# Three of eight key chunks of P·V as products of fp16 halves

## The chip, the cores and the metric

One program runs on one core of a Trainium2 chip. Five engines work side by side and meet only at semaphores: PE (TensorE, the matmuls; its weight loads are listed apart as PEld), ACT (ScalarE), DVE (VectorE), POOL (GpSimd) and SP (SyncE, here only a queue of DMAs). The metric is the device time of one execution in microseconds; less is better.

## What is computed

The reference is one transformer layer on x of shape 4 x 1024 x 128, in fp32: differential attention, then a layer of sixteen gated experts that are mixed through an attention of their own. The change touches the first attention alone:

```python
q = (x @ Wq).reshape(B, T, 2 * H, D).transpose(0, 2, 1, 3) * scaling
dots = jnp.einsum('bhqd,bhkd->bhqk', q, k)
attn_w = jax.nn.softmax(dots.astype(jnp.float32), axis=-1)
attn_w = attn_w[:, :, 0] - lam * attn_w[:, :, 1]
attn = jnp.einsum('bhqk,bhkd->bhqd', attn_w, v)
```

There are 4 batches, 16 softmax heads of 32 columns in 8 pairs that share a V of 64 columns, and 1024 keys.

## The kernel before

The attention is cut into 128 **blocks**: one softmax head against 512 queries (half of a batch's). A **step** `j` has eight blocks (of one batch: four heads times two halves of the queries), so there are 16 steps; four blocks are a **group**. A block has eight **chunks** of 128 keys. For each chunk PE makes S^T = K^T Q in a bank of `st_ps` (three banks, `chunk`, L490, fp16 operands that carry the split parts), ACT takes the exponential into `pT` (L802, fp32), and for each block PE multiplies with V: 32 **units**, unit `n` being 128 queries against one chunk (`values`, L506). A unit is two fp32 matmuls, one for each half of the 128 queries (`TILE_COLS = 64`: the halves lie in different columns of the array), and the trace shows each of them as two passes, so a unit is four MATMUL records. V has a 65th column of ones, which gives the softmax's denominator.

Meanwhile PE computes ahead, through a ring of two pairs of PSUM banks (`ring_ps`), the row maxima of coming groups ("max", L553, emptied by DVE's reduction L1079), the projections of coming steps ("q", "k", "v"), and the transposes and output projection of finished groups ("cols", "project").

Each engine's order is written out. The outer loop is over `kb`; an iteration has eight **slots** `s`. In iteration `kb` PE works at the S chunks of block `kb` two chunks ahead (`ST_AHEAD = 2`), and at P·V of block `kb - 1`:

```python
c = 8 * kb + s + ST_AHEAD
chunk(c)                                   # pe.wait_ge(exp_ok, c - ST_BANKS + 1)
values(kb - 1, sum(PV_SHARE[:s]), sum(PV_SHARE[:s + 1]))   # PV_SHARE = (3, 4, 4, 4, 4, 4, 5, 4)
```

A "max" stands in slots 0, 2, 4 and 6 (in slot 0 ahead of P·V), "q", "k" and "v" at the end of slot 7 of three of a step's eight iterations. ACT does `exponentials(8 * kb + s)` in slot `s`; the first of a block waits until P·V of block `kb - 2` has freed the `pT` buffer (`pv_ok`), and just ahead of it ACT copies that block's sums out of `att_ps` (`raw_copy`, L810, which P·V of the next block waits for). So the chunk of PE's slot 1 waits for the block's first exponential, that of slot 2 for the second, that of slot 3 for the third. POOL combines the heads of a finished group (L386 to L411) and splits q and k of coming steps (L374, L376).

Of the kernel before, what the change touches and what calls it, by code (L numbers as in the profile page):

```python
# [55 lines left out]
SPLIT_PRODUCTS = ((0, 0), (0, 1), (1, 0))  # L56
# [48 lines left out]
EMPTIED = {engine: [emptied(engine, n) for n in range(len(RING) + 1)] for engine in "AV"}  # L105


def block_kernel(nc, x, wq, wkv, wout, lq1, lk1, lq2, lk2, gamma, sim, gates, eq, ek, ev, eo, out):
    ctx = ExitStack()
    with ctx:  # L110
        stack_of = {"memory": ctx}

        def sb(name, shape, dt=F32):
            return stack_of["memory"].enter_context(nc.sbuf_tensor(name, shape, dt))

        def ps(name, shape, dt=F32):
# [61 lines left out]
        st_ps = ps("st_ps", [P, ST_BANKS, HALF])  # L178
        att_ps = ps("att_ps", [P, HALF])
# [42 lines left out]
        weights_in, parts_set = sem("weights_in"), sem("parts_set")  # L222
        ring_ok, ring_A, ring_V = sem("ring_ok"), sem("ring_A"), sem("ring_V")
# [2 lines left out]
        shift_ok = sem("shift_ok")  # L226
        st_ok, exp_ok, pv_ok, raw_ok = sem("st_ok"), sem("exp_ok"), sem("pv_ok"), sem("raw_ok")
        recip_ok, tail_P = sem("recip_ok"), sem("tail_P")
        rms_const_ok = sem("rms_const_ok")
        e_v, e_p, e_a = sem("early_v"), sem("early_p"), sem("early_a")  # L230
        experts_in = sem("experts_in")
# [86 lines left out]
        def _(pool):  # L318
# [23 lines left out]

            pool.memset(v_sb[:, :, :, :, DV:DV1], 1.0).then_inc(parts_set, 1)
            pool.wait_ge(parts_set, 1)
            units = ka[:, :, :, :].rearrange("p a r t -> p (a r t)").bitcast(F32)
            pool.memset(units[K_MAX:K_ALL, :], PAIR_OF_ONE).then_inc(parts_set, 1)
            pool.wait_ge(parts_set, 2)
            pool.memset(units[K_MAX:K_MAX + 1, :], PAIR_OF_UNIT).then_inc(parts_set, 1)
            pool.wait_ge(parts_set, 3)

            def tokens(ap):
                return ap.unsqueeze(2).to_broadcast([P, NT, C])
# [62 lines left out]
            def early(b, stage):  # L415
# [9 lines left out]
                elif stage == 4:  # L425
                    pool.wait_ge(e_v, 8 * (b + 1))
                    pool.tensor_tensor(x2n[:, rows, :], x2c[:, :, :], tokens(gs[:, 0, rows]), ALU.mult).then_inc(g_nP, 1)

            for kb in range(FIRST_BLOCK, END_BLOCK):
                if (kb - 5) % 4 == 0 and 0 <= (kb - 5) // 4 < GROUPS:  # L430
                    combine((kb - 5) // 4)
                if (kb - 6) % 4 == 0 and 0 <= (kb - 6) // 4 < GROUPS:
                    rms((kb - 6) // 4)
                if (kb - 7) % 4 == 0 and 0 <= (kb - 7) // 4 < GROUPS:
                    normalize((kb - 7) // 4)
                for kind, lag in (("q", 13), ("k", 12)):
# [35 lines left out]
        def _(pe):  # L472
# [7 lines left out]
            def chunk(c):  # L480
# [6 lines left out]
                if c >= ST_BANKS:  # L487
                    pe.wait_ge(exp_ok, c - ST_BANKS + 1)
                for k0 in range(0, P, TILE_COLS):
                    mm = pe.matmul(st_ps[k0:k0 + TILE_COLS, c % ST_BANKS, :],  # L490
                                   ka[0:K_ALL, j % 2, r, kt * P + k0:kt * P + k0 + TILE_COLS],
                                   qa[0:K_ALL, j % 2, r, half * HALF:(half + 1) * HALF], start=True, stop=True)
                mm.then_inc(st_ok, 1)

            def values(blk, first, last):

                j, r = blk // 8, blk % 4
                for n in range(first, last):
# [6 lines left out]
                    for q0 in range(0, P, TILE_COLS):
                        mm = pe.matmul(att_ps[q0:q0 + TILE_COLS, qt * DV1:(qt + 1) * DV1],  # L506
                                       pT[:, blk % 2, kt, qt * P + q0:qt * P + q0 + TILE_COLS],
                                       v_sb[:, j % 2, kt, r // 2, :], start=kt == 0, stop=kt == 7)
                if last == 32:
                    mm.then_inc(pv_ok, 1)  # L510

# [64 lines left out]
            for kb in range(FIRST_BLOCK, END_BLOCK):  # L576
                for s in range(8):
                    c = 8 * kb + s + ST_AHEAD
                    if 0 <= c < CHUNKS:
                        if c == 0:  # L580
                            pe.wait_ge(parts_set, 3)
# [25 lines left out]
            for n in range(B):  # L607
# [3 lines left out]
                for t in range(NT):  # L611
                    mm = pe.transpose(gate_ps(n, t // 4)[:, t % 4 * P:(t % 4 + 1) * P], x2n[:, n * NT + t, :], ident[:, :])
# [148 lines left out]
        def _(act):  # L761
# [33 lines left out]
            def exponentials(c):  # L795
                blk, kt = divmod(c, 8)
                act.wait_ge(st_ok, c + 1)
                if c == 0:
                    act.wait_ge(ln_normed, B - 1)
                if kt == 0 and blk >= 2:  # L800
                    act.wait_ge(pv_ok, blk - 1)
                act.activation(pT[:, blk % 2, kt, :], st_ps[:, c % ST_BANKS, :], ACT.Exp).then_inc(exp_ok, 1)  # L802

            def raw_copy(blk):
                g, r = divmod(blk, 4)
# [7 lines left out]
            def empty(op):  # L813
                if "A" not in emptied_by(op):
                    return
                n, kind, which = RING_INDEX[op], op[0], op[1]
                pair = ring_pair(n)
                act.wait_ge(ring_ok, n + 1)
                if kind == "ln":
                    act.activation(xnT[:, which * T:which * T + HALF], pair[:, 0:HALF], ACT.Copy).then_inc(ring_A, 1)  # L820
                elif kind in "qk" and which == 0:
                    act.activation(split[:, 2 * "qk".index(kind), :], pair, ACT.Copy,
                                   scale=QSCALE if kind == "q" else 1.0).then_inc(ring_A, 1)
                elif kind in "qk":
                    if which > 1:
                        act.wait_ge(split_ok, 4 * (which - 2) + 2 * "qk".index(kind) + 2)
                    act.activation(qk_raw[:, "qk".index(kind), :], pair, ACT.Copy,  # L827
                                   scale=QSCALE if kind == "q" else 1.0).then_inc(ring_A, 1)
                elif kind == "v":
                    if which >= 2:  # L830
                        act.wait_ge(pv_ok, 8 * (which - 1))
                    act.activation(v_sb[:, which % 2, :, :, 0:DV], pair.rearrange("p (t h d) -> p t h d", t=NT, h=2),
                                   ACT.Copy).then_inc(ring_A, 1)
                else:
                    act.activation(attn_nT[:, :, :].rearrange("p t q -> p (t q)"), pair[:, 0:HALF], ACT.Copy).then_inc(ring_A, 1)
# [494 lines left out]
```

## Time and profile before

| | us |
|---|---|
| median of 3 runs | 1598.44 (1597.79 to 1598.49) |
| the profiled execution, its own time | 1597.66 |
| span of its trace | 1595.9 |
| busy: PE, PEld | 1481.9, 1181.1 |
| busy: DVE, ACT, POOL | 996.2, 851.8, 500.4 |
| attention blocks, first to last copy of sums | 102.3 to 1184.9 |

The busy times are shares of the whole span; the first hundred microseconds prepare the inputs, and what comes after the blocks is the expert layer, which the change doesn't touch. Within the blocks the clock of TensorE is granted in full. The trace gives every instruction a start and a duration; a duration of a matmul holds the time through the array too, so that matmuls in a row overlap, and their rate is read from the distance of their starts.

### The profile page before, as it was taken

The numbers are of one execution on the slowest core, as the hardware profiler recorded it, in microseconds if no ns is written. First come the engines' busy times: TensorE is split into PE (matmuls) and PEld (weight loads), VectorE is DVE, ScalarE is ACT, GpSimd is POOL, SyncE is SP. The second block draws the span as 40 slices with busy tenths as digits, with TensorE's granted clock in tenths as the row PEclk, the third lists the DMA queues.
The fourth block names the chain that finished last, engine by engine and source line by source line (L and its number), as shares of the span: only waits on it lengthen the run. The fifth ranks groups of instructions, "written<-read, shape, count | busy, mean of one in ns | idle before, by whom it ended". The sixth has DMA issues, their size and how long they took to land. (4 is left out here: it accounts for less than half of the span.)

```text
span 1595.9 us, 56507 instructions
## 1 busy us (share of the span) xinstructions
PE 1481.9 (93%) x25266; PEld 1181.1 (74%) x25266; DVE 996.2 (62%) x1375; ACT 851.8 (53%) x1693; POOL 500.4 (31%) x432
## 2 busy tenths in 40 slices
PE   2699999999999999999999999999972899999997
PEld 1267777777777777777777777777762799989997
DVE  5576665756666666676656667666407466666665
ACT  2056555555655556565565655555643455555553
POOL 4202333232333323333332333332232433333230
PEclk9689999999999999999999999999985999999999
DMA  3101010110101011010100101010002000000000
GB/s 101 45 17 43 8 37 17 28 32 13 43 11 35 20 25 32 13 42 12 33 22 23 32 13 42 13 33 3 3 2 53 1 8 9 8 7 8 8 8 9
DMA packets 37036, 36.46 MB, mean 23 GB/s; under 512 B 14272, under 2 KB 24256, under 8 KB 36800
## 3 DMA queue, kind: packets, MB, share of 16 engines
q1 hardware_dynamic: 36288, 32.62, 8.6%
q8 instruction: 201, 3.29, 0.9%
q10 hardware_dynamic: 512, 0.26, 0.1%
q14 instruction: 35, 0.29, 0.1%
HBM read 5.33 MB, written 2.10 MB: 5 GB/s over the span
## 5 line engine op out<-in xcount | busy, mean ns | idle before, releaser
L1079 DVE TENSOR_REDUCE part_max<-ring_ps 128x2 f32<-128x1024 f32 x512 | 625.1, 1224 | 366.1 <-PE ring_ps L553 357.3
L506 PEld LDWEIGHTS att_ps<-v_sb,pT 128*64 128x64 f32 x16384 | 631.3, 138 | 145.4 <-issue 30.2
L506 PE MATMUL att_ps<-v_sb,pT 128*64 128x65 f32 x16384 | 650.9, 222 | 2.5 <-issue 2.5
L802 ACT ACTIVATE pT<-st_ps 128x512 f32<-128x512 f32 x1024 | 553.7, 608 | 170.3 <-PE st_ps L490 166.7
L490 PE MATMUL st_ps<-qa,ka 98*64 98x512 f16 x2048 | 398.9, 387 | 0.0
L553 PE MATMUL ring_ps<-ka,qa 96*64 96x512 f16 x2048 | 313.6, 386 | 26.2 <-DMA ka<-split 19.1
L460 POOL TENSOR_TENSOR xs<-xnT,rw_all 128x2048 f32 (+1 forms) x32 | 115.5, 3610 | 206.9 <-PE t_ps L653 200.1
L490 PEld LDWEIGHTS st_ps<-qa,ka 98*64 98x64 f16 x2048 | 115.2, 109 | 76.7 <-issue 27.7
L810 ACT ACTIVATE raw_attn<-att_ps 128x260 f32<-128x260 f32 x128 | 49.5, 387 | 205.6 <-PE att_ps L506 205.6
L667 PE MATMUL qkv_ps<-ew_split,xsT 128*128 128x192 f16 x1536 | 142.9, 247 | 4.2 <-DVE xsT L1247 4.2
L553 PEld LDWEIGHTS ring_ps<-ka,qa 96*64 96x64 f16 x2048 | 96.1, 113 | 56.7 <-issue 24.6
L667 PEld LDWEIGHTS qkv_ps<-ew_split,xsT 128*128 128x128 f16 x1536 | 127.1, 98 | 7.7 <-DVE xsT L1247 5.8
L1247 DVE TENSOR_TENSOR xsT<-t_ps,xsT 128x512 f16<-128x512 f32 x128 | 82.5, 686 | 50.6 <-ACT xsT L906 50.4
L386 POOL TENSOR_TENSOR recips<-recips,lam 128x8 f32<-128x8 f32 x32 | 6.5, 202 | 332.6 <-DVE recips L1112 332.6
L906 ACT ACTIVATE xsT<-t_ps 128x512 f16<-128x512 f32 x128 | 70.2, 603 | 66.1 <-PE t_ps L653 66.1
L653 PE MATMUL t_ps<-ident,xs 128*128 128x128 f32 x512 | 67.3, 275 | 24.8 <-POOL xs L460 22.7
L399 POOL TENSOR_TENSOR tl<-tl,rms_const 128x8 f32<-128x8 f32 x32 | 6.5, 203 | 261.9 <-DVE tl L1116 261.9
L653 PEld LDWEIGHTS t_ps<-ident,xs 128*128 128x128 f32 x512 | 56.9, 142 | 25.1 <-issue 25.1
L411 POOL TENSOR_TENSOR attn_n<-attn,tl 128x256 f32<-128x256 f32 x64 | 37.9, 613 | 94.8 <-DVE tl L1120 94.8
L376 POOL TENSOR_TENSOR split<-qk_raw,split 128x1024 f16<-128x1024 f32 x30 | 63.9, 2131 | 2.4
L389 POOL TENSOR_TENSOR scaled<-raw_attn,recips 128x1024 f32<-128x1024 f32 x32 | 60.9, 1903 | 2.5
L827 ACT ACTIVATE qk_raw<-ring_ps 128x1024 f32<-128x1024 f32 x30 | 30.7, 1023 | 55.3 <-PE ring_ps L541 55.3
(193 smaller groups left out, 1359.1 us busy)
## 6 DMA issues: line engine op xcount, KB each, us to landing
qa<-split SPq DMA_DIRECT2D x192, 64.0 KB, 2.0
ka<-split SPq DMA_DIRECT2D x192, 64.0 KB, 2.0
resid<-in_L_attn_x SPq DMA_DIRECT2D x4, 512.0 KB, 6.9
out<-yo SPq DMA_DIRECT2D x32, 64.0 KB, 1.5
qa<-shift_rows ACTq DMA_DIRECT2D x64, 4.0 KB
wkv_sb<-in_L_attn_Wkv SPq DMA_DIRECT2D x1, 512.0 KB, 5.0
ew<-in_L_ffn_q_proj SPq DMA_DIRECT2D x1, 512.0 KB, 5.5
ew<-in_L_ffn_k_proj SPq DMA_DIRECT2D x1, 512.0 KB, 7.2
```

The costliest lines, as they stand in the source:

```text
L376: pool.tensor_tensor(split[:, 2 * n + 1, :], qk_raw[:, n, :], split[:, 2 * n, :], ALU.subtract).then_inc(split_ok, 1)
L389: pool.tensor_tensor(scaled[:, :, :, :], raw_attn[:, buf, :, :, 0:DV], recips[:, buf, :, :].unsqueeze(3).to_broadcast([P, 4, 4, DV]), ALU. ...
L460: pool.tensor_tensor(xs[:, r, :, :], x2n[:, bass.ds(m, 1), :].to_broadcast([P, E, C]), rw_all[:, bass.ds(m, 1), :].rearrange("p a e -> p e ...
L490: mm = pe.matmul(st_ps[k0:k0 + TILE_COLS, c % ST_BANKS, :], ka[0:K_ALL, j % 2, r, kt * P + k0:kt * P + k0 + TILE_COLS], qa[0:K_ALL, j % 2, ...
L506: mm = pe.matmul(att_ps[q0:q0 + TILE_COLS, qt * DV1:(qt + 1) * DV1], pT[:, blk % 2, kt, qt * P + q0:qt * P + q0 + TILE_COLS], v_sb[:, j % ...
L553: mm = pe.matmul(pair[c0:c0 + TILE_COLS, sub * HALF:(sub + 1) * HALF], qa[0:K_MAX, j % 2, r, q0 + c0:q0 + c0 + TILE_COLS], ka[0:K_MAX, j % ...
L653: mm = pe.transpose(t_ps[:, bank, e * P:(e + 1) * P], xs[:, t % 2, 4 * group + e, :], ident[:, :])
L667: mm = pe.matmul(qkv_ps[:, 0:3 * DE], xsT[:, t % 2, x_part, e, :], ew_split[:, w_part, e, :], start=e == 0 and n == 0, stop=e == E - 1 and ...
L802: act.activation(pT[:, blk % 2, kt, :], st_ps[:, c % ST_BANKS, :], ACT.Exp).then_inc(exp_ok, 1)
L906: act.activation(xsT[:, t % 2, 0, 4 * group:4 * group + 4, :], t_ps[:, group % 2, :].rearrange("p (e q) -> p e q", e=4), ACT.Copy).then_in ...
L1079: dve.tensor_reduce(part_max[:, which % 2, 2 * quarter + m // 2, m % 2, :], pair.rearrange("p (n k) -> p n k", n=2), AX.X, ALU.max, negate ...
L1247: dve.tensor_tensor(xsT[:, t % 2, 1, 4 * group:4 * group + 4, :], t_ps[:, group % 2, :].rearrange("p (e q) -> p e q", e=4), xsT[:, t % 2, ...
```

## The change

For chunks 0, 1 and 2 of each block ACT takes the exponential twice: into `pT` in fp32, as before, and into `p_half[..., 0, ...]` in fp16. Only the second raises `exp_ok`. POOL subtracts the one from the other, which gives the remainder, `p_half[..., 1, ...]` in fp16. V is copied twice as well (fp32 and fp16, ACT) and its remainder taken by POOL once a step. P·V of these chunks is then three fp16 products, high·high, high·low and low·high (`SPLIT_PRODUCTS = ((0, 0), (0, 1), (1, 0))`), each for both halves of the queries, so six fp16 matmuls in a unit in place of two fp32 ones with two passes each. Units are taken in the order of chunks 3 to 7, 0 to 2. The exponentials get a bias of ln 1024, against fp16's small range; it falls out of the quotient.

```diff
+SPLIT_CHUNKS = 3
+KT_ORDER = tuple(range(SPLIT_CHUNKS, 8)) + tuple(range(SPLIT_CHUNKS))
+EXP_SCALE = 1024.0
...
+            def low_halves(blk):
+
+                for kt in range(SPLIT_CHUNKS):
+                    pool.wait_ge(wide_ok, SPLIT_CHUNKS * blk + kt + 1)
+                    pool.wait_ge(exp_ok, 8 * blk + kt + 1)
+                    pool.tensor_tensor(p_half[:, blk % 2, 1, kt, :], pT[:, blk % 2, kt, :], p_half[:, blk % 2, 0, kt, :],
+                                       ALU.subtract).then_inc(low_ok, 1)
+
+            def low_values(j):
...
+                pool.tensor_tensor(v_half[:, j % 2, 1, :, :, 0:DV], v_sb[:, j % 2, :, :, 0:DV], v_half[:, j % 2, 0, :, :, 0:DV],
+                                   ALU.subtract).then_inc(v_low_ok, 1)
+
             for kb in range(FIRST_BLOCK, END_BLOCK):
+                if 0 <= kb < BLOCKS:
+                    low_halves(kb)
+                if (kb + 1) % 8 == 0 and 0 <= (kb + 1) // 8 < STEPS:
+                    low_values((kb + 1) // 8)
...
-                    qt, kt = divmod(n, 8)
+                    qt, kt = n // 8, KT_ORDER[n % 8]
...
+                    if n == 8 - SPLIT_CHUNKS:
+                        pe.wait_ge(v_low_ok, 2 * (j + 1))
+                        pe.wait_ge(low_ok, SPLIT_CHUNKS * (blk + 1))
+                    opens, closes = n % 8 == 0, n % 8 == 7
+                    if kt >= SPLIT_CHUNKS:
...
+                    else:
+                        for k, (p_part, v_part) in enumerate(SPLIT_PRODUCTS):
+                            cols = DV if v_part else DV1
+                            for q0 in range(0, P, TILE_COLS):
+                                mm = pe.matmul(att_ps[q0:q0 + TILE_COLS, qt * DV1:qt * DV1 + cols],
+                                               p_half[:, blk % 2, p_part, kt, qt * P + q0:qt * P + q0 + TILE_COLS],
+                                               v_half[:, j % 2, v_part, kt, r // 2, 0:cols], start=False,
+                                               stop=closes and k == 2)
...
-                act.activation(pT[:, blk % 2, kt, :], st_ps[:, c % ST_BANKS, :], ACT.Exp).then_inc(exp_ok, 1)
+                wide = act.activation(pT[:, blk % 2, kt, :], st_ps[:, c % ST_BANKS, :], ACT.Exp, bias=exp_bias[:, 0:1])
+                if kt < SPLIT_CHUNKS:
+                    wide.then_inc(wide_ok, 1)
+                    act.activation(p_half[:, blk % 2, 0, kt, :], st_ps[:, c % ST_BANKS, :], ACT.Exp,
+                                   bias=exp_bias[:, 0:1]).then_inc(exp_ok, 1)
+                else:
+                    wide.then_inc(exp_ok, 1)
```

ACT's order around a block in whose start the v projection is copied, before (L810 copies the sums, L802 are the exponentials, L832 copies v):

```order
L810 ACTIVATE raw_attn<-att_ps 128x260 [waits pv_ok]
L802 ACTIVATE pT<-st_ps 128x512 [waits pv_ok,st_ok]
L832 ACTIVATE v_sb<-ring_ps 128x16x64 [waits pv_ok,ring_ok]
L802 ACTIVATE pT<-st_ps 128x512 [waits st_ok] x7
L810 ACTIVATE raw_attn<-att_ps 128x260 [waits recip_ok,tail_P,pv_ok]
```

and with the change (L860 is the copy of the sums, L846 the fp32 and L849 the fp16 exponential, L882 and L884 the two copies of v):

```order
L860 ACTIVATE raw_attn<-att_ps 128x260 [waits pv_ok]
L846 ACTIVATE pT<-st_ps,exp_bias 128x512 [waits pv_ok,st_ok]
L849 ACTIVATE p_half<-st_ps,exp_bias 128x512
L882 ACTIVATE v_sb<-ring_ps 128x16x64 [waits pv_ok,ring_ok]
L884 ACTIVATE v_half<-ring_ps 128x16x64
L846 ACTIVATE pT<-st_ps,exp_bias 128x512 [waits st_ok]
L849 ACTIVATE p_half<-st_ps,exp_bias 128x512
L846 ACTIVATE pT<-st_ps,exp_bias 128x512 [waits st_ok]
L849 ACTIVATE p_half<-st_ps,exp_bias 128x512
L846 ACTIVATE pT<-st_ps,exp_bias 128x512 [waits st_ok] x5
```

Each of the first three exponentials has a second one behind it, and there are two copies of v between the first and the second chunk's.

PE's order in slots 0 to 2 of a quiet iteration, before, from the first P·V unit on (L490 is a chunk of S, L553 a "max"):

```order
L506 MATMUL att_ps<-v_sb,pT 64x65 [waits ring_A,raw_ok,exp_ok]
L506 MATMUL att_ps<-v_sb,pT 64x65 x5
L490 MATMUL st_ps<-qa,ka 64x512 [waits exp_ok]
L490 MATMUL st_ps<-qa,ka 64x512
L506 MATMUL att_ps<-v_sb,pT 64x65 x8
L490 MATMUL st_ps<-qa,ka 64x512 [waits exp_ok]
L490 MATMUL st_ps<-qa,ka 64x512
L506 MATMUL att_ps<-v_sb,pT 64x65 x8
L553 MATMUL ring_ps<-ka,qa 64x512 [waits ring_V]
L553 MATMUL ring_ps<-ka,qa 64x512 x3
L490 MATMUL st_ps<-qa,ka 64x512 [waits exp_ok]
```

and with the change (L520 is the chunk of S, L541 the fp32 units, L548 the fp16 ones):

```order
L541 MATMUL att_ps<-v_sb,pT 64x65 [waits ring_A,raw_ok,exp_ok]
L541 MATMUL att_ps<-v_sb,pT 64x65 x5
L520 MATMUL st_ps<-qa,ka 64x512 [waits exp_ok]
L520 MATMUL st_ps<-qa,ka 64x512
L541 MATMUL att_ps<-v_sb,pT 64x65 x4
L548 MATMUL att_ps<-v_half,p_half 64x65 [waits low_ok,v_low_ok]
L548 MATMUL att_ps<-v_half,p_half 64x65
L548 MATMUL att_ps<-v_half,p_half 64x64 x2
L548 MATMUL att_ps<-v_half,p_half 64x65 x4
L548 MATMUL att_ps<-v_half,p_half 64x64 x2
L548 MATMUL att_ps<-v_half,p_half 64x65 x2
L520 MATMUL st_ps<-qa,ka 64x512 [waits exp_ok]
```

Slot 1 now has two fp32 units and two fp16 ones of six matmuls each; the first fp16 matmul of a block waits for POOL. The chunk of the next slot stands behind them, with the same wait for `exp_ok` as before.

## Rows read from the trace of the kernel before

**Rows 1.** The page: span, busy time, slices with the granted clock.

```profile
span 1595.9 us, 56507 instructions
...
PE 1481.9 (93%) x25266; PEld 1181.1 (74%) x25266; DVE 996.2 (62%) x1375; ACT 851.8 (53%) x1693; POOL 500.4 (31%) x432
...
PEclk9689999999999999999999999999985999999999
...
```

**Rows 2.** Busy time of every engine over the attention blocks.

```profile
...
core 0: us, PE busy (x) PEld busy (x) DVE busy (x) ACT busy (x) POOL busy (x), PEclk, DMA share, GB/s
102.30:1184.90 1082.60, 1079.49 (x21045) 827.82 (x21045) 683.50 (x754) 637.91 (x1217) 341.84 (x344) 1.00 0.10 23
...
```

**Rows 3.** Instructions that touch raw_attn: durations, first and last start.

```profile
...
L810 ACT ACTIVATE raw_attn<-att_ps x128: 387/387/388, 102.3 to 1184.9; 128x260 f32<-128x260 f32 x128
...
```

**Rows 4.** Timeline from the start of a quiet block, T = 850.19.

```profile
...
850.19 0.39 ACT L810 ACTIVATE raw_attn<-att_ps 128x260 f32<-128x260 f32 x1 [1.80 <-PE att_ps L506]
850.19 0.60 PE L553 MATMUL ring_ps<-ka,qa 96*64 96x512 f16 x4
850.47 2.55 ACT L802 ACTIVATE pT<-st_ps 128x512 f32<-128x512 f32 x5
...
850.67 0.57 PE L506 MATMUL att_ps<-v_sb,pT 128*64 128x65 f32 x12
...
851.11 0.41 PE L490 MATMUL st_ps<-qa,ka 98*64 98x512 f16 x2
...
851.35 0.63 PE L506 MATMUL att_ps<-v_sb,pT 128*64 128x65 f32 x16
...
851.82 0.38 PE L490 MATMUL st_ps<-qa,ka 98*64 98x512 f16 x2
...
852.94 0.38 PE L490 MATMUL st_ps<-qa,ka 98*64 98x512 f16 x2
...
```

**Rows 5.** Matmuls by form: busy us, mean ns of one.

```profile
...
L506 PE MATMUL att_ps<-v_sb,pT 128*64 128x65 f32 x16384 | 650.9, 222 | 2.5 <-issue 2.5
...
L603 PE MATMUL qkv_ps<-simn_split,x2T 128*128 128x16 f16 x96 | 3.2, 175 | 6.3 <-DVE x2T L1159 6.3
...
```

**Rows 6.** Weight loads by form: busy us, mean ns of one.

```profile
...
L506 PEld LDWEIGHTS att_ps<-v_sb,pT 128*64 128x64 f32 x16384 | 631.3, 138 | 145.4 <-issue 30.2
...
L490 PEld LDWEIGHTS st_ps<-qa,ka 98*64 98x64 f16 x2048 | 115.2, 109 | 76.7 <-issue 27.7 <-ACT pT L802 0.9
...
L561 PEld LDWEIGHTS ring_ps<-identh,shift 128*8 128x8 f16 x128 | 6.6, 86 | 3.8 <-DVE part_max L1079 1.6
...
```

**Rows 7.** Timeline of PE where 24 short fp16 matmuls run in a row.

```profile
...
1203.67 0.81 PE L603 MATMUL qkv_ps<-simn_split,x2T 128*128 128x16 f16 x24 [0.24 <-DVE x2T L1159]
...
```

**Rows 8.** Timeline of a block with a q projection, T = 874.69.

```profile
...
876.59 1.02 ACT L827 ACTIVATE qk_raw<-ring_ps 128x1024 f32<-128x1024 f32 x1 [1.02 <-PE ring_ps L541]
...
877.51 2.06 ACT L802 ACTIVATE pT<-st_ps 128x512 f32<-128x512 f32 x4
...
878.19 0.39 PE L490 MATMUL st_ps<-qa,ka 98*64 98x512 f16 x2
...
```

**Rows 9.** Timeline of the block with the v projection, T = 893.90.

```profile
...
895.87 1.02 ACT L832 ACTIVATE v_sb<-ring_ps 128x1024 f32<-128x1024 f32 x1 [1.09 <-PE ring_ps L536]
...
896.79 2.06 ACT L802 ACTIVATE pT<-st_ps 128x512 f32<-128x512 f32 x4
...
897.47 0.39 PE L490 MATMUL st_ps<-qa,ka 98*64 98x512 f16 x2
...
```

**Rows 10.** POOL by form: busy us, mean ns of one.

```profile
...
L376 POOL TENSOR_TENSOR split<-qk_raw,split 128x1024 f16<-128x1024 f32 x30 | 63.9, 2131 | 2.4
...
L394 POOL TENSOR_TENSOR attn_sq<-attn 128x512 f32<-128x512 f32 x32 | 33.3, 1040 | 2.5
...
```

**Rows 11.** ACT by form: fp32 and fp16 results of one width.

```profile
...
L802 ACT ACTIVATE pT<-st_ps 128x512 f32<-128x512 f32 x1024 | 553.7, 608 | 170.3 <-PE st_ps L490 166.7
L906 ACT ACTIVATE xsT<-t_ps 128x512 f16<-128x512 f32 x128 | 70.2, 603 | 66.1 <-PE t_ps L653 66.1
...
```

More of the change, by code:

```diff
@@ L157, in block_kernel @@
         pT = sb("pT", [P, 2, NT, HALF])
+        p_half = sb("p_half", [P, 2, 2, SPLIT_CHUNKS, HALF], F16)
+        v_half = sb("v_half", [P, 2, 2, NT, 2, DV1], F16)
+        exp_bias = sb("exp_bias", [P, 1])
         part_max = sb("part_max", [P, 2, 8, 2, 2])
@@ L228, in block_kernel @@
         recip_ok, tail_P = sem("recip_ok"), sem("tail_P")
+        wide_ok, low_ok, v_low_ok = sem("wide_ok"), sem("low_ok"), sem("v_low_ok")
         rms_const_ok = sem("rms_const_ok")
@@ L344, in _ @@
             pool.wait_ge(parts_set, 1)
+            pool.memset(v_half[:, :, 0, :, :, DV:DV1], 1.0).then_inc(parts_set, 1)
+            pool.wait_ge(parts_set, 2)
+            pool.memset(exp_bias[:, :], math.log(EXP_SCALE)).then_inc(parts_set, 1)
+            pool.wait_ge(parts_set, 3)
             units = ka[:, :, :, :].rearrange("p a r t -> p (a r t)").bitcast(F32)
             pool.memset(units[K_MAX:K_ALL, :], PAIR_OF_ONE).then_inc(parts_set, 1)
-            pool.wait_ge(parts_set, 2)
+            pool.wait_ge(parts_set, 4)
             pool.memset(units[K_MAX:K_MAX + 1, :], PAIR_OF_UNIT).then_inc(parts_set, 1)
-            pool.wait_ge(parts_set, 3)
+            pool.wait_ge(parts_set, 5)
             def tokens(ap):
@@ L427, in early @@
                     pool.tensor_tensor(x2n[:, rows, :], x2c[:, :, :], tokens(gs[:, 0, rows]), ALU.mult).then_inc(g_nP, 1)
+            def low_halves(blk):
[5 more added lines that the diff above has]
+            def low_values(j):
+                pool.wait_ge(v_low_ok, 2 * j + 1)
+                pool.wait_ge(ring_A, EMPTIED["A"][RING_INDEX["v", j] + 1])
+                pool.tensor_tensor(v_half[:, j % 2, 1, :, :, 0:DV], v_sb[:, j % 2, :, :, 0:DV], v_half[:, j % 2, 0, :, :, 0:DV],
+                                   ALU.subtract).then_inc(v_low_ok, 1)
             for kb in range(FIRST_BLOCK, END_BLOCK):
+                if 0 <= kb < BLOCKS:
+                    low_halves(kb)
+                if (kb + 1) % 8 == 0 and 0 <= (kb + 1) // 8 < STEPS:
+                    low_values((kb + 1) // 8)
                 if (kb - 5) % 4 == 0 and 0 <= (kb - 5) // 4 < GROUPS:
@@ L504, in values @@
                         pe.wait_ge(ring_A, EMPTIED["A"][RING_INDEX["v", j] + 1])
[L505 to L508, printed above, removed]
+                    if n == 8 - SPLIT_CHUNKS:
[4 more added lines that the diff above has]
+                        for q0 in range(0, P, TILE_COLS):
+                            mm = pe.matmul(att_ps[q0:q0 + TILE_COLS, qt * DV1:(qt + 1) * DV1],
+                                           pT[:, blk % 2, kt, qt * P + q0:qt * P + q0 + TILE_COLS],
+                                           v_sb[:, j % 2, kt, r // 2, :], start=opens, stop=closes)
+                    else:
+                        for k, (p_part, v_part) in enumerate(SPLIT_PRODUCTS):
+                            cols = DV if v_part else DV1
+                            for q0 in range(0, P, TILE_COLS):
+                                mm = pe.matmul(att_ps[q0:q0 + TILE_COLS, qt * DV1:qt * DV1 + cols],
+                                               p_half[:, blk % 2, p_part, kt, qt * P + q0:qt * P + q0 + TILE_COLS],
+                                               v_half[:, j % 2, v_part, kt, r // 2, 0:cols], start=False,
+                                               stop=closes and k == 2)
                 if last == 32:
@@ L580, in _ @@
                         if c == 0:
-                            pe.wait_ge(parts_set, 3)
+                            pe.wait_ge(parts_set, 5)
                         chunk(c)
@@ L799, in exponentials @@
                     act.wait_ge(ln_normed, B - 1)
+                    act.wait_ge(parts_set, 3)
                 if kt == 0 and blk >= 2:
                     act.wait_ge(pv_ok, blk - 1)
-                act.activation(pT[:, blk % 2, kt, :], st_ps[:, c % ST_BANKS, :], ACT.Exp).then_inc(exp_ok, 1)
+                wide = act.activation(pT[:, blk % 2, kt, :], st_ps[:, c % ST_BANKS, :], ACT.Exp, bias=exp_bias[:, 0:1])
[5 more added lines that the diff above has]
+                    wide.then_inc(exp_ok, 1)
             def raw_copy(blk):
@@ L832, in empty @@
                     act.activation(v_sb[:, which % 2, :, :, 0:DV], pair.rearrange("p (t h d) -> p t h d", t=NT, h=2),
+                                   ACT.Copy).then_inc(v_low_ok, 1)
+                    act.activation(v_half[:, which % 2, 0, :, :, 0:DV], pair.rearrange("p (t h d) -> p t h d", t=NT, h=2),
                                    ACT.Copy).then_inc(ring_A, 1)
```

## The prediction

> **What bounds the kernel now.** The page comes first [rows 1]: PE is busy for 93% of the span, no other engine for more than 62%, and the granted clock stands at 9 tenths or more in every slice between the preparation and the expert layer. The change lies in the attention blocks alone, so the second view is the busy time in that stretch [rows 2]: PE 1079.49 of 1082.60 us, clock 1.00 (the upper level, 2.4 GHz), ACT 637.91, POOL 341.84. Their length per block comes from the first and the last copy of the sums, 102.3 and 1184.9, 127 blocks apart [rows 3]: 8.52 us. A PE that is busy everywhere says nothing yet of waits, because durations of matmuls overlap. So the third view is the timeline from the start of a block [rows 4]; I call T the start of the copy of the sums. ACT starts its first exponential 0.28 us after T, and the five in a row take 2.55 us, the last 0.6 of it, so they start (2.55 - 0.60) / 4 = 0.48 us apart. The first ends at 850.47 + 0.60 = 851.07, and the chunk of slot 1 starts on PE at 851.11. It could hardly start later without a stall: this is the place where ACT and PE meet in every block. From there PE runs on its own pace: slot 1 takes 851.82 - 851.11 = 0.71 us, slot 2 with its "max" 1.12 us.
>
> **What PE saves.** A fp32 unit is four records, two passes over two halves of the array. Sixteen of them take 0.63 us from the first start to the last end [rows 4], one lasts 0.222 [rows 5], so the eight pairs start (0.63 - 0.222) / 7 = 0.058 us apart and a unit costs 0.116. No trace row has fp16 matmuls of 65 columns in two halves. The nearest is the fp16 pair of 512 columns: two pairs in a "max" take 0.60 and one lasts 0.38, so a pair takes 0.22 [rows 4], 0.42 ns a column and some 4 ns over. Sixty-five such columns are 27 + 4 = 31 ns (the fp32 pass, 58, is twice the columns' time and the same 4). Three pairs make a fp16 unit of 0.093: **-0.023** a unit, 12 units a block. Where a fp32 unit follows a fp16 one, its weights load while only a short matmul covers it. A load of 8 columns takes 86 ns, of 64 fp16 columns 109, of 64 fp32 columns 138 [rows 6]: fp32 weights occupy 138 - 86 = 52 ns, a fp16 matmul covers 30 of them, and this happens three times a block (inside slots 2, 4 and 6): **+0.075** in all, rounded up. The bounds of the unit: below, 24 fp16 matmuls of 16 columns with their loads take 0.81 us, the last 0.175 of it [rows 5, 7], so they start 27.7 ns apart, and if two halves go in one such interval a unit is 3 x 27.7 = 0.083. Above, if this interval is a limit on each load and matmul, whichever half they go to, it is 6 x 27.7 = 0.166. I take 0.093, because rows 4 have the same layout (64 columns of weights, two halves) and differ in length alone.
>
> The Trainium skill speaks against my value. "TensorE: Matmul & The Clock Gate", section "LDWEIGHTS (loading the stationary operand)", has a weight load take its column count over 1.2 GHz, 53 ns for 64 columns of either type; a unit would then be about 3 x 56 = 0.168 us. The loads of rows 6 disagree: 109 - 86 = 23 ns for 56 columns more is 2.4 GHz.
>
> **What ACT adds.** An exponential with a fp16 result has no row of its own, but a fp16 copy of the same width takes 603 ns against the exponential's 608 [rows 11]; so each second one costs a pitch of 0.48. The chunks of slots 1, 2 and 3 wait for `exp_ok`, which now comes with the second. In a quiet block, counted from T:
> - first pair: starts at 0.28 and 0.76, ends at 1.36, the chunk starts at 1.41 (0.04 to 0.05 later, as in rows 4). Before 0.92: **+0.49**.
> - second pair: 1.24 and 1.72, ends 2.32, chunk 2.37. PE gets there at 1.41 + 0.71 - 2 x 0.023 = 2.07 and waits 0.30. Before it was 1.63: +0.74 up to here.
> - third pair: 2.20 and 2.68, chunk not before 3.33. PE comes at 2.37 + 1.12 = 3.49; no wait, and from here ACT, at 0.48 a chunk against PE's 0.7 to 1.1 a slot, catches up.
>
> The other ten fp16 units of the block give back 0.23, the loads take 0.075: a quiet block is 0.74 - 0.155 = **+0.585** longer. Five of eight blocks are of this kind.
>
> In the two blocks with a q or a k projection the copy of it, 1.02 us, stands between the first and the second exponential [rows 8] (the k block repeats them). The first pair is early enough; the second starts at 877.51 and 877.99, its chunk at 878.64, where it was 878.19: +0.45, less 0.155: **+0.295** each. In the v block there are now two copies. The second begins 0.92 after the first (895.87 to 896.79) [rows 9]; the exponentials begin at 897.71 and 898.19, the chunk at 898.84, where it was 897.47: +1.37, less 0.155: **+1.215**. Slot 2's "max" needs v's bank of the ring, free with the second copy at 896.79 + 1.02 = 897.81, well ahead.
>
> Eight blocks: 5 x 0.585 + 2 x 0.295 + 1.215 = 4.73, or 0.591 a block, and 128 of them 75.7 us. The profiled execution took 1597.66 us, 0.8 below the median of the runs shown and 1.8 over its span; 1597.7 + 75.7 = 1673.4, against the median **1674 us**.
>
> **Costed at nothing.** POOL's subtraction in fp32 and fp16 with a fp16 result takes 2131 ns for 1024 columns [rows 10], so about 1.07 for 512. The third of a block ends at T + 3.3 + 1.1 = 4.4, and PE asks for it in slot 1 of the next iteration, 9 us after T. POOL's work is 341.84 / 127 = 2.7 a block, and the change adds three subtractions a block and an eighth of V's: 3 x 1.07 + 2.13 / 8 = 3.5, together 6.2 of 9.1 us. Behind the waiting subtraction stand POOL's combination and splitting of other groups, whose readers (PE's "cols", SP's DMAs) come several iterations later. If that cover goes, see the second rival. The added memsets at the start and the bias operand are below what I can price; the two added waits of PE in slot 1 stand behind fp32 units that cover them.
>
> **The rivals.**
> - *The fp16 unit costs 0.166.* For it: the 27.7 ns of rows 7 is the fastest rate at which any row has whole load-and-matmul pairs in a row, and even the fp32 pairs come at only 58 / 2 = 29. Against it: the two halves start together in rows 4 (a pair of 512 columns takes as long as one would). Units become 0.050 dearer, loads are covered; slot 1 stays hidden behind ACT. Quiet block 0.74 + 0.50 = 1.24, q and k 0.95, v 1.87: 9.97 / 8 x 128 = 159.5, or **1758 us**. The skill's load time, above, would end there too. Chance 20%; 7% more for a unit between the two (1700 to 1745).
> - *POOL becomes the bound.* If a subtraction of 512 columns took the 2.13 us that rows 10 have for 1024, POOL had 3 x 2.13 + 0.27 + 2.7 = 9.4 us a block, and with the gaps in its chains about 9.6; 128 x (9.6 - 8.52) = 138, or **1736 us**. It decides from about 2.0 us a subtraction. Against it: the row L394, 512 columns at 1040 ns, and the DVE work beside it reads PSUM. ("GPSIMD Engine Reference", section "Key points", of the Trainium skill has POOL share its SBUF interfaces with DVE when DVE has two SBUF inputs; no row here shows POOL slowed by it.) Chance 6%.
> - *Faster: the waits of the chunks cost nothing,* because PE lets the P·V matmuls behind a waiting chunk go ahead of it. Then only PE's work counts: 12 x 0.023 - 0.075 = 0.20 a block, -26 us, **1573 us**. It decides where the added waits are under 0.2 us a block. Against it: in rows 4 the P·V of slot 1 starts after the chunk that waited, not before. Chance 5%.
>
> The forecast keeps 62%; its own range is 1650 to 1700. The lower end is the unit of 0.083 without the loads' 0.075: quiet 0.74 - 0.33 = 0.41, q and k 0.12, v 1.04, 3.33 / 8 x 128 = 53. The whole range must take in the dear unit: 1650 to 1758. A measurement of this kernel tells about 0.2% from no change. Slower by more holds all but the last rival and what I have not thought of: 93%; faster 5%, within 0.2% the remaining 2%.
>
> **What would show it.** In the profile after: the chunk of slot 1 of a quiet block at T + 1.4 and that of slot 2 at T + 2.4, each right behind the end of a fp16 exponential; waits of PE for ACT where there were hardly any; blocks of 9.1 us on average, the v block longest; six fp16 records in some 93 ns; PE's busy time in the stretch below its length. Wrong would be: fp16 records 27 ns apart one by one, POOL's subtractions of over 2 us with PE waiting for them, or a slot 1 that starts at T + 0.9 as before.

## The result, and the profile after

The changed kernel takes **1724.38 us** (median of 4 runs, 1723.32 to 1725.17) against 1598.47 for the one before beside it: ratio 1.079, 95% interval 1.0774 to 1.0806. The forecast of slower was right, and the whole range, 1650 to 1758, held it. But the likeliest value, 1674, was 50 us low, and the forecast's own range, 1650 to 1700, did not reach so far: the wider one was there for a dear matmul unit that this kernel doesn't have, so that it held the result is luck.

The page of the changed kernel, beside [rows 1]: PE's share falls to 87%, ACT and POOL rise by 307 and 474 us of work, and the granted clock stays where it was.

```profile
span 1722.9 us, 63981 instructions
...
PE 1499.2 (87%) x28338; PEld 1153.5 (67%) x28338; DVE 1002.2 (58%) x1375; ACT 1159.1 (67%) x2093; POOL 974.8 (57%) x834
...
PEclk8699999999999999999999999999997699999999
```

The copies of the sums, now L860, are 127 blocks apart from 103.4 to 1308.7, beside [rows 3]: (1308.7 - 103.4) / 127 = 9.49 us a block in place of 8.52. 127 x 0.97 = 123 of the 126 us are in the attention blocks.

```profile
L860 ACT ACTIVATE raw_attn<-att_ps x128: 387/387/389, 103.4 to 1308.7; 128x260 f32<-128x260 f32 x128
```

The timeline from the start of a quiet block (one in whose start no q, k or v is copied), T = 932.23, answers to [rows 4]:

```profile
932.23 0.39 ACT L860 ACTIVATE raw_attn<-att_ps 128x260 f32<-128x260 f32 x1 [1.59 <-PE att_ps L548]
...
932.51 0.68 ACT L846 ACTIVATE pT<-st_ps,exp_bias 128x512 f32<-128x512 f32 x1
...
932.72 0.57 PE L541 MATMUL att_ps<-v_sb,pT 128*64 128x65 f32 x12
933.08 0.69 ACT L849 ACTIVATE p_half<-st_ps,exp_bias 128x512 f16<-128x512 f32 x1
933.65 0.70 ACT L846 ACTIVATE pT<-st_ps,exp_bias 128x512 f32<-128x512 f32 x1
...
933.82 0.41 PE L520 MATMUL st_ps<-qa,ka 98*64 98x512 f16 x2 [0.54 <-ACT p_half L849]
...
934.22 0.71 ACT L849 ACTIVATE p_half<-st_ps,exp_bias 128x512 f16<-128x512 f32 x1
...
934.79 0.71 ACT L846 ACTIVATE pT<-st_ps,exp_bias 128x512 f32<-128x512 f32 x1
...
934.98 0.41 PE L520 MATMUL st_ps<-qa,ka 98*64 98x512 f16 x2 [0.33 <-ACT p_half L849]
...
935.36 0.72 ACT L849 ACTIVATE p_half<-st_ps,exp_bias 128x512 f16<-128x512 f32 x1
...
935.93 1.31 ACT L846 ACTIVATE pT<-st_ps,exp_bias 128x512 f32<-128x512 f32 x2
...
936.13 0.41 PE L520 MATMUL st_ps<-qa,ka 98*64 98x512 f16 x2
```

The order of events is the one worked out: pairs of exponentials, and the chunks of slots 1 and 2 (L520 at 933.82 and 934.98) each right behind the end of the fp16 one (933.08 + 0.69 = 933.77; 934.22 + 0.71 = 934.93). What is off is the step between exponentials: 932.51, 933.08, 933.65, **0.57** us, where the sum had 0.48. So the chunks come at T + 1.59 and T + 2.75, not at 1.41 and 2.37; and the third pair, which was to be free, now just holds the chunk of slot 3 too (935.36 + 0.72 = 936.08, chunk at 936.13; over blocks 17 to 111 it starts 0.053 us behind that end in blocks of every kind). The groups of ACT and POOL, by form, beside [rows 10, 11]:

```profile
L846 ACT ACTIVATE pT<-st_ps,exp_bias 128x512 f32<-128x512 f32 x1024 | 670.8, 711 | 77.9 <-PE st_ps L520 77.9
L849 ACT ACTIVATE p_half<-st_ps,exp_bias 128x512 f16<-128x512 f32 x384 | 270.1, 703 | 0.0
```

```profile
L446 POOL TENSOR_TENSOR p_half<-pT,p_half 128x512 f16<-128x512 f32 x384 | 443.6, 1159 | 303.1 <-ACT p_half L849 299.6 <-issue 1.4
```

An exponential of 512 columns lasts 711 ns where it lasted 608. POOL's subtraction, 1159 ns, is near the 1070 of the sum. The waits, first POOL's for ACT and then PE's for ACT, of which there were hardly any before:

```profile
POOL p_half L446 <- ACT p_half L849: 299.6, 138, 12.6
...
PEld st_ps L520 <- ACT p_half L849: 196.7, 366, 1.5
...
PE st_ps L520 <- ACT p_half L849: 108.7, 214, 1.4
```

Finer than any one block: the mean time from the chunk of each slot to the next one, over blocks 17 to 111, worked out from the starts of the S matmuls of both traces, changed kernel less the one before (us).

```
              slot 0   slot 1   slot 2   slot 3   slots 4 to 7
quiet         +0.658   +0.449   +0.035   -0.021   -0.11
q, k           0.000   +0.629   +0.035   -0.020   -0.10
v              0.000   +1.543   +0.035   -0.024   -0.11
```

### The profile page after: what moved, and what is told of

The parts are those of the page before. It is cut to its first block and busy times, and to the rows that moved or that the text cites. A ratio compares the mean times of both kernels' runs of the same rounds, so it can differ in the third digit from the quotient of the medians.

```text
span 1722.9 us, 63981 instructions
## 1 busy us (share of the span) xinstructions
PE 1499.2 (87%) x28338; PEld 1153.5 (67%) x28338; DVE 1002.2 (58%) x1375; ACT 1159.1 (67%) x2093; POOL 974.8 (57%) x834
## 5 line engine op out<-in xcount | busy, mean ns | idle before, releaser
L846 ACT ACTIVATE pT<-st_ps,exp_bias 128x512 f32<-128x512 f32 x1024 | 670.8, 711 | 77.9 <-PE st_ps L520 77.9
L446 POOL TENSOR_TENSOR p_half<-pT,p_half 128x512 f16<-128x512 f32 x384 | 443.6, 1159 | 303.1 <-ACT p_half L849 299.6
L520 PE MATMUL st_ps<-qa,ka 98*64 98x512 f16 x2048 | 404.4, 392 | 108.9 <-ACT p_half L849 108.7
L541 PEld LDWEIGHTS att_ps<-v_sb,pT 128*64 128x64 f32 x10240 | 428.7, 138 | 101.6 <-issue 29.0
L541 PE MATMUL att_ps<-v_sb,pT 128*64 128x65 f32 x10240 | 482.9, 224 | 2.3 <-issue 2.3
L548 PE MATMUL att_ps<-v_half,p_half 128*64 128x65 f16 (+1 forms) x9216 | 294.0, 195 | 0.0
L548 PEld LDWEIGHTS att_ps<-v_half,p_half 128*64 128x64 f16 x9216 | 254.8, 111 | 39.6 <-issue 0.2
L520 PEld LDWEIGHTS st_ps<-qa,ka 98*64 98x64 f16 x2048 | 114.5, 109 | 238.8 <-ACT p_half L849 196.7
L849 ACT ACTIVATE p_half<-st_ps,exp_bias 128x512 f16<-128x512 f32 x384 | 270.1, 703 | 0.0
L490 POOL TENSOR_TENSOR xs<-xnT,rw_all 128x2048 f32 (+1 forms) x32 | 115.5, 3610 | 210.1 <-PE t_ps L696 203.3
L860 ACT ACTIVATE raw_attn<-att_ps 128x260 f32<-128x260 f32 x128 | 49.5, 387 | 172.1 <-PE att_ps L548 172.1
```

What stands on the lines that cost most here:

```text
L446: pool.tensor_tensor(p_half[:, blk % 2, 1, kt, :], pT[:, blk % 2, kt, :], p_half[:, blk % 2, 0, kt, :], ALU.subtract).then_inc(low_ok, 1)
L490: pool.tensor_tensor(xs[:, r, :, :], x2n[:, bass.ds(m, 1), :].to_broadcast([P, E, C]), rw_all[:, bass.ds(m, 1), :].rearrange("p a e -> p e ...
L520: mm = pe.matmul(st_ps[k0:k0 + TILE_COLS, c % ST_BANKS, :], ka[0:K_ALL, j % 2, r, kt * P + k0:kt * P + k0 + TILE_COLS], qa[0:K_ALL, j % 2, ...
L548: mm = pe.matmul(att_ps[q0:q0 + TILE_COLS, qt * DV1:qt * DV1 + cols], p_half[:, blk % 2, p_part, kt, qt * P + q0:qt * P + q0 + TILE_COLS], ...
L846: wide = act.activation(pT[:, blk % 2, kt, :], st_ps[:, c % ST_BANKS, :], ACT.Exp, bias=exp_bias[:, 0:1])
L849: act.activation(p_half[:, blk % 2, 0, kt, :], st_ps[:, c % ST_BANKS, :], ACT.Exp, bias=exp_bias[:, 0:1]).then_inc(exp_ok, 1)
```

## The experiments

Theory A: the mechanism of the prediction is whole, and its sum lacks one thing, the bias operand, which lengthens each of ACT's exponentials. Theory B: PE's fp16 units or POOL's subtractions cost more than reckoned. The first four kernels ran on one chip, beside a kernel before of 1598.2 us, the next four on another, beside 1597.63 us.

**The changed kernel without the bias operand.**

```diff
-                wide = act.activation(pT[...], st_ps[...], ACT.Exp, bias=exp_bias[:, 0:1])
+                wide = act.activation(pT[...], st_ps[...], ACT.Exp)
```

and the same for the second one.

> The changed kernel with its exponentials taken without the bias operand (so P is not scaled by 1024; nothing else differs). Theory A, the bias operand accounts for what my sum left out: the pitch of the exponentials falls back from 0.57 to 0.48 us and the time to the sum's 1674 us, give or take 5. Theory B, what was left out is dearer P V units on PE or late subtractions on POOL: the time stays within 5 us of 1724.

1680.65 us, ratio 1.0513 (1.0491 to 1.0534): 44 us less than with the bias. Its exponentials by form:

```profile
L846 ACT ACTIVATE pT<-st_ps 128x512 f32<-128x512 f32 x1024 | 589.6, 631 | 121.2 <-PE st_ps L520 119.5 <-DVE part_max L1130 1.5
L849 ACT ACTIVATE p_half<-st_ps 128x512 f16<-128x512 f32 x384 | 239.4, 623 | 0.0
```

631 ns in place of 711. Its slots against the kernel before: quiet 0.480 and 0.273 in slots 0 and 1 (the sum had 0.49 and 0.30 - 0.05 = 0.25), q and k 0.452 (0.45), v 1.369 (1.37). The exponentials of a row start 0.478 us apart, where they started 0.569 apart with the bias (medians of the trace). B falls, and A holds but for its size: the case that the sum was made for, 1674 give or take 5, came out 6 to 7 us above it.

**The bias alone, on the kernel before.**

```diff
-                act.activation(pT[...], st_ps[...], ACT.Exp).then_inc(exp_ok, 1)
+                act.activation(pT[...], st_ps[...], ACT.Exp, bias=exp_bias[:, 0:1]).then_inc(exp_ok, 1)
```

> The kernel before with nothing but the bias operand on its exponentials (P scaled by 1024, which falls out). Each exponential then lasts some 0.70 us and starts 0.57 after the one before. By A the chunk of slot 1 comes 0.1 us later after each start of a block, that of slot 2 at T + 0.28 + 0.57 + 0.70 + 0.05 = 1.60 against T + 1.63 now, so 0.1 us a block and in all 1611 us (1605 to 1616). By B the bias is hidden: within 3 us of 1598.5.

1608.72 us, ratio 1.0062 (1.0039 to 1.0086): 10.5 us, in the range given. Each quiet block is 0.09 us longer, all in slot 0, q, k and v blocks 0.08 in slots 1 and 2.

```profile
L806 ACT ACTIVATE pT<-st_ps,exp_bias 128x512 f32<-128x512 f32 x1024 | 640.2, 694 | 124.1 <-PE st_ps L493 123.9
```

694 against 608. The price of the operand depends on how many exponentials stand between T and the chunk that waits: one here (10 us), two and then four in the changed kernel (44 us).

**The second exponential alone, on the kernel before.**

```diff
-                act.activation(pT[...], st_ps[...], ACT.Exp).then_inc(exp_ok, 1)
+                wide = act.activation(pT[...], st_ps[...], ACT.Exp)
+                if kt < 3:
+                    act.activation(p_half[:, blk % 2, 0, kt, :], st_ps[...], ACT.Exp).then_inc(exp_ok, 1)
+                else:
+                    wide.then_inc(exp_ok, 1)
```

> The kernel before with the second, fp16 exponential of chunks 0 to 2 (no bias), whose result nobody reads; P V stays in fp32, POOL and V as before. By my sum (0.49 + 0.25 in a quiet block, 0.45 in those with q, k or v): (5 x 0.74 + 3 x 0.45) / 8 x 128 = 81 us, so 1679 us. If the waits of the chunks were not on the path it would stay at 1598.

1683.47 us, ratio 1.0535 (1.0512 to 1.0557): +85 where 81 was expected. PE, POOL and V are as before here, so the waits of the chunks by themselves make the change slow. Slots: quiet 0.490 and 0.273, q, k and v 0.452. Slot 2 is 0.022 us longer in all blocks, though the chunk of slot 3 starts 0.215 us behind the third fp16 exponential and so waits for nothing. The kernel with the bias alone has the same 0.022 in slot 2 of its q, k and v blocks, whose chunk of slot 2 waits for ACT, and 0.000 in the quiet ones, whose doesn't. So the slot behind a chunk that had to wait is 0.02 us longer; why was not followed.

```profile
PEld st_ps L491 <- ACT p_half L805: 121.6, 365, 0.8
...
PE st_ps L491 <- ACT p_half L805: 42.0, 125, 0.4
```

**The fp16 units alone.** P and V of the split chunks are constants, so their part of P·V is left out of the result; ACT and POOL work as in the kernel before:

```diff
-                if kt < SPLIT_CHUNKS:
-                    wide.then_inc(wide_ok, 1)
-                    act.activation(p_half[...], st_ps[...], ACT.Exp).then_inc(exp_ok, 1)
-                else:
-                    wide.then_inc(exp_ok, 1)
+                wide.then_inc(exp_ok, 1)
...
-                if 0 <= kb < BLOCKS:
-                    low_halves(kb)
```

> The changed kernel's P V on PE alone: the fp16 halves of P and V are constants written once, ACT takes every exponential once and without a bias, POOL subtracts nothing (so P V of chunks 0 to 2 is left out of the result). By my sum 12 x 0.023 - 0.075 = 0.20 us a block less: 1573 us. By the rival of the dear unit (0.166 us) 12 x 0.05 = 0.6 a block more: 1675 us.

1583.72 us, ratio 0.9911 (0.989 to 0.9932), 11 us above the 1573 expected. Its blocks go from 109.3 to 1168.8, 8.343 us each, 0.182 less than before (the sum: 0.20), 23 us in all; some 7 of them are lost ahead of the blocks, which start at 109.3 in place of 102.3, where this kernel, and only this one, sets the whole of both half buffers. PE's timeline:

```profile
854.38 0.26 PE L543 MATMUL att_ps<-v_half,p_half 128*64 128x65 f16 x6
854.48 0.54 PE L536 MATMUL att_ps<-v_sb,pT 128*64 128x65 f32 x12
...
855.74 0.36 PE L543 MATMUL att_ps<-v_half,p_half 128*64 128x65 f16 x12
855.93 0.39 PE L516 MATMUL st_ps<-qa,ka 98*64 98x512 f16 x2
856.15 0.26 PE L543 MATMUL att_ps<-v_half,p_half 128*64 128x65 f16 x6
856.24 0.66 PE L536 MATMUL att_ps<-v_sb,pT 128*64 128x65 f32 x16
```

Twelve fp16 matmuls in 0.36 us, one lasting 0.19 (six pairs): (0.36 - 0.19) / 5 = 0.034 by these rounded rows, and one unit, from its start in slot 2 to the fp32 units behind it, takes 856.24 - 856.15 = 0.09; from the unrounded starts a pair is 31 ns and a unit 0.093 to 0.094 (the sum: 0.093). The rival of the unit at 0.166 us is out. "TensorE: Matmul & The Clock Gate", section "LDWEIGHTS (loading the stationary operand)", of the Trainium skill would have a load of 64 columns take 53 ns; the trace does not agree, with one load a half every 31 ns.

**Deferred halves, factor in the shift.** If the waits are the cost, they can go: the fp32 exponential alone releases the chunk, ACT copies the fp16 half from `pT` in SBUF in slots 2 to 4 (V's in slot 6), and the factor 1024 is added to the scores' shift by one small DVE instruction a group.

```diff
-                    act.activation(p_half[...], st_ps[...], ACT.Exp, bias=...).then_inc(exp_ok, 1)
+                wide.then_inc(exp_ok, 1)
+            def high_half(blk, kt):
+                act.wait_ge(exp_ok, 8 * blk + kt + 1)
+                act.activation(p_half[:, blk % 2, 0, kt, :], pT[:, blk % 2, kt, :], ACT.Copy).then_inc(wide_ok, 1)
...
+                        if 2 <= s < 2 + SPLIT_CHUNKS:
+                            high_half(kb, s - 2)
...
+                dve.tensor_scalar(shift32[:, buf, :, :], shift32[:, buf, :, :], math.log(EXP_SCALE), None, ALU.add)
```

> The changed kernel with both causes taken away: the factor 1024 is added to the shift of the scores by a small DVE instruction a group, so that no exponential has a bias operand, and the fp16 halves of P and V are copied by ACT from the fp32 ones in SBUF, P's in slots 2 to 4, V's in slot 6, so that the fp32 exponential alone releases the chunks of S. If pitch and waits are all that made the change slow, what is left is PE's saving, 0.18 us a block as the kernel with constant halves showed: 1598 - 23 = 1575 us (1570 to 1582). If the doubled ACT work or POOL's subtractions cost something by themselves, it stays over 1598.

1587.72 us, ratio 0.9935 (0.992 to 0.9949): faster than the kernel before, by 10 us, and 137 us faster than the changed kernel. The bias has gone too, so the deferral is better read against the changed kernel without it (1680.65): 93 us, with the same PE work and ACT and POOL within 2 us of busy time. ACT's timeline from the start of a quiet block:

```profile
857.49 0.39 ACT L863 ACTIVATE raw_attn<-att_ps 128x260 f32<-128x260 f32 x1 [1.68 <-PE att_ps L548]
857.77 1.57 ACT L846 ACTIVATE pT<-st_ps 128x512 f32<-128x512 f32 x3
859.20 0.65 ACT L851 ACTIVATE p_half<-pT 128x512 f16<-128x512 f32 x1
859.72 0.62 ACT L846 ACTIVATE pT<-st_ps 128x512 f32<-128x512 f32 x1
860.20 0.66 ACT L851 ACTIVATE p_half<-pT 128x512 f16<-128x512 f32 x1
860.72 0.63 ACT L846 ACTIVATE pT<-st_ps 128x512 f32<-128x512 f32 x1
861.20 0.67 ACT L851 ACTIVATE p_half<-pT 128x512 f16<-128x512 f32 x1
```

Three exponentials (L846) run ahead of the first copy (L851), and PE's waits for ACT's exponentials between 200 and 1000 us, 129.8 and 70.5 us in the changed kernel, have shrunk to this row:

```profile
PEld st_ps L520 <- ACT pT L846: 3.4, 20, 0.2
```

It is still 12 us above the 1575 expected, and outside the 1570 to 1582 given. Against the kernel with constant halves its blocks are 0.087 us longer, 11 us in all, and most of it can be placed. In three iterations (`kb` = 40, 72, 104, where POOL also prepares the second layer's norm) slot 3 with its "cols" takes 2.49 us in place of 1.32 and slot 1 is 0.34 longer, of which slot 4 of the next iteration gives 0.5 back: 3 us. In the iterations behind a new shift, a quarter of all, slot 4 is 0.123 us longer, 29 times: 3.6 us. The next kernel, without the added DVE instruction, does not have this, so it is the price of that instruction. The last six iterations, which have no "max" left to cover ACT, lose 2.5 us: there chunks of slots 4 to 6 start 0.05 us behind the exponential that they wait for. The first iteration loses 1.0 us. In slot 1 of every second of the iterations behind a new shift DVE shows something else: its small instruction L1164, 16 elements from two SBUF inputs, lasts 0.90 us and ends as POOL's L406 does (895.95 + 0.90 = 896.85; 895.76 + 1.06 = 896.82).

```profile
895.76 1.06 POOL L406 TENSOR_TENSOR attn_sq<-attn 128x512 f32<-128x512 f32 x1
...
895.95 0.90 DVE L1164 SCALAR_TENSOR_TENSOR shift<-shift 128x16 f16<-128x16 f16 x1
```

Its minimum, median and maximum here, and then those of the same instruction (L1145) in the kernel with constant halves:

```profile
L1164 DVE SCALAR_TENSOR_TENSOR shift<-shift x32: 174/177/897, 78.7 to 1130.6; 128x16 f16<-128x16 f16 x32
```

```profile
L1145 DVE SCALAR_TENSOR_TENSOR shift<-shift x32: 174/176/177, 86.3 to 1127.7; 128x16 f16<-128x16 f16 x32
```

The instruction added ahead of it has moved it under one of POOL's, 14 times of 32, and all 14 end 0.030 to 0.033 us behind it; but slot 4 is 0.12 longer at the other places just as well, so these 0.7 us fall into slack. Some 1.5 us of the blocks were not placed.

**Deferred halves, bias kept.** The same edit without the DVE instruction; the exponentials keep `bias=exp_bias[:, 0:1]`.

> The same deferral, but the exponentials keep the bias operand. It costs what it cost the kernel before, some 10 us, once it is not doubled: 1586 us. If the bias weighs as much as between the changed kernel and the one without bias (44 us), 1619 us.

1608.76 us, ratio 1.0068 (1.0051 to 1.0085): a miss for both numbers. It is 21 us slower than with the factor in the shift, and as the 3.6 us of the DVE instruction have gone, the bias costs some 25 us here, neither 10 nor 44. 0.09 us a block are those of the kernel with the bias alone; besides, slot 5 of the iterations `kb` = 3 and 7 (mod 8) is 0.35 us longer, 11 us in all over a quarter of the blocks. The trace puts the wait of the chunk behind it down to ACT's exponential, which stands behind the three copies, here in `kb` = 83:

```profile
816.20 0.41 PE L520 MATMUL st_ps<-qa,ka 98*64 98x512 f16 x2 [0.24 <-ACT pT L846]
```

Without the bias this chunk started 0.14 us (`kb` = 3 mod 8) and 0.25 us (7 mod 8) behind the end of the same exponential, with it 0.14 us in both. So ACT had little or no slack left there, and the longer exponentials ahead of it go to PE. The exponentials are long again, the copies are not:

```profile
L846 ACT ACTIVATE pT<-st_ps,exp_bias 128x512 f32<-128x512 f32 x1024 | 667.9, 705 | 20.8 <-PE st_ps L520 17.7
L851 ACT ACTIVATE p_half<-pT 128x512 f16<-128x512 f32 x384 | 249.9, 651 | 0.0
```

**Fewer changes from fp16 to fp32 weights.** In every second query tile the fp16 units come first.

```diff
-                    qt, kt = n // 8, KT_ORDER[n % 8]
+                    qt = n // 8
+                    kt = KT_ORDER[n % 8] if qt % 2 == 0 else KT_ORDER[(n + 8 - SPLIT_CHUNKS) % 8]
...
-                                               v_half[:, j % 2, v_part, kt, r // 2, 0:cols], start=False,
+                                               v_half[:, j % 2, v_part, kt, r // 2, 0:cols], start=opens and k == 0,
```

> The deferred kernel without bias, with the fp16 units first in every second query tile, so that a block has two changes from fp16 to fp32 weights in place of three. Each is 0.027 us in the trace of the kernel with constant halves: 3.5 us less than the deferred kernel. If that gap is no cost of the change of weights, no difference.

1583.91 us, ratio 0.9913 (0.9898 to 0.9927), 3.8 us under the kernel without it on the same chip; expected 3.5. The intervals of the ratios overlap, since both hold the noise of the kernel before, but the five times of each don't (1583.14 to 1585.48 against 1586.95 to 1588.81), and per block the traces give 8.395 against 8.430, 4.4 us.

**Four chunks in halves.** `SPLIT_CHUNKS = 4` on top.

> As the one before, with four chunks in halves. PE saves four units of 0.022 a block more, 11 us. POOL then has 4 x 1.16 + 0.27 + 2.7 = 7.6 us of work in a block of 8.2: if its chains leave no gaps it is 11 us faster than with three; if POOL binds, PE waits for it in slot 1 and it is slower than with three.

1592.94 us, ratio 0.9966 (0.9953 to 0.9979), 9 us slower than with three. Most iterations save 0.04 to 0.09 us (expected: 0.09), but one in eight (`kb` = 2 mod 8) loses 0.2, and the three with the second layer's norm on POOL (`kb` = 40, 72, 104) lose 2.3, 4.1 and 2.3 us, as much as the whole difference. Two rows of PE's waits between 200 and 1000 us, both absent in the changed kernel; the second names POOL:

```profile
PEld att_ps L549 <- issue: 8.4, 10, 2.3
...
PE att_ps L549 <- POOL p_half L446: 6.7, 3, 2.2
```

**Copies earlier where ACT issues DMAs**, and the kernel without that edit again, on another chip beside 1597.27 us.

```diff
+                        first = 1 if kb % 4 == 2 else 2
+                        if first <= s < first + SPLIT_CHUNKS:
+                            high_half(kb, s - first)
```

> The deferred kernel with alternating order, and in the blocks in which ACT issues the two DMAs of the shift (some 1.25 us in slot 6) the three copies to fp16 stand in slots 1 to 3 in place of 2 to 4. The deferred kernel's blocks of this kind are 0.15 to 0.3 us longer than those of the kernel with constant halves. If the copies crowd the DMAs there, a quarter of the blocks gets some 0.1 to 0.2 us back, 3 to 6 us in all, 1578 to 1581 us. If not, it stays at 1584.

> The deferred kernel with alternating order once more, beside the one with earlier copies on the same chip: 1584 us.

1584.64 us (1582.96 to 1585.6) against 1582.69 (1579.78 to 1584.19), ratios 0.9915 (0.9901 to 0.9928) and 0.9903 (0.9888 to 0.9918): no gain; no slot of the two traces differs by more than 0.015 us in blocks 17 to 111. So the copies in slots 2 to 4 do not crowd the DMAs. The best version is thus the one with alternating order: 1.0% under the kernel before (0.9903), 0.9% on the chip before (0.9913).

## Why the prediction was right, and where it was short

- **The place.** PE and ACT meet at the chunk of slot 1, and the second exponential pushes it: shown by the second exponential alone (+85 us) and by its deferral (-93 us without the bias, -116 with it).
- **PE's saving.** Unit 0.093 to 0.094 us (0.093), block 0.182 (0.20): right. Slots 2 to 7 were to give back 0.155 us. They give 0.14 in a quiet block with constant halves, 0.12 in the changed kernel without the bias, and 0.09 in the changed kernel itself, where the third pair holds the chunk of slot 3. Without the bias that is 0.035 x 128 = 4 us of the 6 to 7 by which the sum was low there.
- **ACT's waits.** Right for q, k, v and quiet blocks at the pitch of 0.48, within 0.03 us each, as the kernel without bias shows.
- **The step that failed: "the bias operand [is] below what I can price".** It is the term that was mis-sized: taken as 0, it is 44 us of the 50. It works through the path that the sum had: two exponentials stand ahead of the chunk of slot 1, four ahead of that of slot 2, each 0.09 us later. The trace of the kernel before had a row to price it by, which I did not read: the expert layer's exponential of 512 columns has such an operand, `nm`, and takes 692 ns against 608 for the one without. (It also sums its row, so this row alone doesn't single out the operand; the 694 ns of the kernel with the bias alone do.)

```profile
L935 ACT ACTIVATE p<-s_ps,nm 128x512 f32<-128x512 f32 x4 | 2.8, 692 | 0.0
```

The Trainium skill has the same: "ScalarE: Activation LUTs", section "What ACT_TABLE_LOAD costs", says that each per-partition pointer operand adds about 93 ns. The traces agree nearly: 694 - 608 = 86 on the kernel before, 711 - 631 = 80 on the changed one, and 0.57 - 0.48 = 0.09 of pitch. With 0.57 in the sum, slot 0 of a quiet block is 1.59 - 0.92 = 0.67 (0.658 measured) and slot 1 ends at T + 2.75.
- **The rivals.** The dear unit was refuted by the constant halves. POOL did not bind in the changed kernel; with four chunks it holds PE up in three iterations, at 1.16 us a subtraction. That PE lets P·V overtake a waiting chunk was refuted by the waits and by the 85 us of the second exponential alone. The measured time falls where the prediction had a unit between the two prices (1700 to 1745, 7%), and by no such unit: that the whole range held it was luck, as the sum's own bounds did not.

## What to carry to other kernels

When a second instruction is put behind one whose completion another engine waits for, ask which of the two has to raise the semaphore: here the extra work cost 85 us on the path, and from the copy in SBUF, two slots later, with POOL's work and one more DVE instruction, 11 us against constant halves. Price every operand that an edit adds, the small ones on a repeated instruction first, from any row of the trace that has it, however far from the change. A cheaper operation on the bound engine (0.2 us a block) was worth less here than what it waits for (0.75 to 1.1 in a quiet block).

## What the runs showed of the hardware

- An exponential of 512 columns with a per-partition bias operand starts 0.57 us after the one before it, without it 0.48.
- Two halves of 64 weight columns with 64 or 65 moving fp16 columns go in 31 ns a pair, six loads and six matmuls in 0.093 to 0.094 us; so there is one load and one matmul every 16 ns, and the 27.7 ns of [rows 7], measured with 128 weight columns, is no limit on each of them when they take turns on two halves.
- A chunk of S that had to wait for ACT made its slot 0.02 us longer than one that came in time (slot 2 of the kernel with the bias alone: 0.022 in q, k and v blocks, 0.000 in quiet ones).
- A DVE instruction of 16 elements with two SBUF inputs lasted up to 897 ns instead of 176, ending 0.03 us after the POOL instruction that ran beside it, which took 1060 ns in place of 1040. "GPSIMD Engine Reference", section "Key points", of the Trainium skill names this sharing, and the trace agrees, with DVE as the one that waits; here it cost nothing that the slots show.
